# Ramp and tail orders, three moved steps and an idle TensorE, in a fused attention and expert kernel

## The reference

```
x = x + tanh(g_xattn) * (cross_attention(layernorm(x), ctx) @ Wo + bo)     # 16 heads of 8, 120 keys
h = rms(layernorm(x)) ;  q, k = rms per head of h @ wq.T, h @ wk.T ; v = h @ wv.T
y = layernorm(x) + causal_attention(q, k, v) @ wo.T   (features 0..31 of the attention part are zero)
gates = the top 2 of 4 of softmax(rms(y) @ gate_w.T), made to sum to 1
x = x + tanh(g_ffn) * (y + sum over 4 experts of gate * expert(rms(y)))    (features 0..31 of the experts are zero)
```

## Time and profile before

| | us |
|---|---|
| median of three executions (lowest, highest) | 1125.39 (1122.77, 1125.41) |
| the profiled execution | 1120.12 |
| its span, first to last instruction | 1118.4 |
| TensorE (PE) busy | 1010.6, 90% |
| VectorE (DVE) busy | 806.0, 72% |
| ScalarE (ACT) busy | 734.0, 66% |
| GpSimd (POOL) busy | 334.9, 30% |
| steps -1, 0, 1 begin at | 0, 34.6, 67.6 |
| step 2 and the loop begin at | 103.3, 160.3 |
| one round of the loop | 64.1 |
| steps 15, 16, 17, 18 begin at | 931.8, 994.5, 1054.8, 1098.6 |

### The profile page before, as it was taken

How to read it: one execution, slowest core, us unless ns; L and a number is a source line. 1 busy time by engine, 2 the same in 40 slices (tenths; PEclk the granted TensorE clock), 3 DMA queues, 4 the chain that set the end, 5 groups by cost and what they waited for, 6 DMA issues and landing times.

```text
span 1118.4 us, 25981 instructions
## 1 busy us (share of the span) xinstructions
PE 1010.6 (90%) x8578; PEld 622.6 (56%) x8578; DVE 806.0 (72%) x2170; ACT 734.0 (66%) x1331; POOL 334.9 (30%) x458
## 2 busy tenths in 40 slices
PE   3657799999999999999999999999999999998897
PEld 1334456656565655656565565655565565555454
DVE  7457777777877777787778777787777778655423
ACT  3455667676776766677676667768676767765453
POOL 6422314051422414151331405142241415132120
PEclk9979899999999999999999999999999999999899
DMA  6426533454433334454333344443333444403100
GB/s 193 111 48 185 142 94 71 117 126 123 126 104 98 101 85 111 123 126 123 100 102 87 87 122 126 123 121 102 97 92 89 125 123 112 118 9 93 33 10 10
DMA packets 77156, 114.26 MB, mean 102 GB/s; under 512 B 7616, under 2 KB 40000, under 8 KB 76992
## 3 DMA queue, kind: packets, MB, share of 16 engines
q1 hardware_dynamic: 76752, 111.54, 38.2%
q10 hardware_dynamic: 368, 2.24, 0.6%
HBM read 58.97 MB, written 53.74 MB: 101 GB/s over the span
## 4 chain that ended last, share of the span: by engine, by line
PE 56%; DVE 23%; ACT 10%; issue 8%; DMA 2%; POOL 0%; DVEq 0%; SPq 0%; ACTq 0%; POOLq 0%
PE ps_pv L1161 9%; PE ps_w L1187 7%; PE ps_s2a L1140 6%; PE ps_s2a L1198 5%; PE ps_s2b L1140 4%; PE ps_s2b L1205 4%; ACT probs L787 4%; DVE mpadB L915 4%; PE ps_t L1044 4%; DVE mpadA L915 3%; PE ps_w L1205 3%; PE ps_t L1174 2%; PE ps_w L1122 2%; PE ps_w L1118 2%; DVE ym L944 2%
## 5 line engine op out<-in xcount | busy, mean ns | idle before, releaser
L787 ACT ACTIVATE probs<-ps_s2a 120x512 f32<-120x512 f32 (+1 forms) x256 | 153.7, 600 | 92.3 <-PE ps_s2a L1140 86.8
L915 DVE TENSOR_REDUCE mpadB<-ps_w 128x4 f32<-128x512 f32 x256 | 158.6, 682 | 29.0 <-PE ps_w L1122 29.0
L915 DVE TENSOR_REDUCE mpadA<-ps_w 128x4 f32<-128x480 f32 x252 | 147.8, 649 | 36.7 <-PE ps_w L1122 36.6
L787 ACT ACTIVATE probs<-ps_s2b 120x512 f32<-120x512 f32 (+1 forms) x256 | 154.0, 602 | 0.0
L678 POOL TENSOR_SCALAR_AFFINE_SELECT probs<-probs 128x1024 f32<-128x1024 f32 x128 | 139.8, 1092 | 0.1
L1187 PE MATMUL ps_w<-W,hid 128*128 128x96 f32 x1024 | 130.0, 281 | 4.4 <-DVE split_k L821 1.1
L1187 PEld LDWEIGHTS ps_w<-W,hid 128*128 128x128 f32 x1024 | 122.2, 195 | 16.4 <-issue 13.5
L649 POOL TENSOR_TENSOR rB<-vrB,neg_half 128x4 f32<-128x4 f32 x16 | 16.1, 1007 | 374.1 <-DVE veB L814 374.1
L1140 PE MATMUL ps_s2a<-qdA,kstA 128*120 128x512 f32 x128 | 69.3, 541 | 14.9 <-issue 7.9
L944 DVE SCALAR_TENSOR_TENSOR ym<-ps_w,gates,ym 128x96 f32<-128x96 f32 x192 | 47.6, 310 | 43.6 <-PE ps_w L1187 43.5
L1198 PE MATMUL ps_s2a<-hid,W 128*128 128x512 f32 x160 | 78.4, 604 | 0.0
(11 more groups left out here) (202 smaller groups left out, 2086.4 us busy)
## 6 DMA issues: line engine op xcount, KB each, us to landing
scratch_Aq<-split_q SPq DMA_DIRECT2D x48, 256.0 KB, 2.4
qdA<-scratch_Aq SPq DMA_DIRECT2D x64, 192.0 KB
scratch_Bq<-split_q SPq DMA_DIRECT2D x48, 256.0 KB, 2.4
scratch_Bk<-split_k SPq DMA_DIRECT2D x48, 256.0 KB, 3.0
qdB<-scratch_Bq SPq DMA_DIRECT2D x64, 192.0 KB
kstB<-scratch_Bk SPq DMA_DIRECT2D x64, 192.0 KB
scratch_Ak<-split_k SPq DMA_DIRECT2D x48, 240.0 KB, 2.3
kstA<-scratch_Ak SPq DMA_DIRECT2D x64, 180.0 KB
```

Of the source, the lines that this page charges most:

```text
L787: nc.scalar.activation(probs[0:k, slot_of(part, *index), :], bank[0:k, :], ACT.Exp, scale=SCALE if part == "A" else 1.0).then_inc(done, 1)
L915: nc.vector.tensor_reduce(mneg[OP[part]][:, :, c, b], bank[:, 0:HT * k].rearrange("p (h k) -> p h k", h=HT), AX.X, ALU.max, negate=True).t ...
```

## The change

In the loop three works move. `base` becomes a work of A and goes from `first_experts` to the end of `self_attention`, so that it now runs for the group whose attention comes next in the same step; the load of x of the next group stands at the head of the step as before and waits for it. The context has a work of its own, `N ctx`, behind it. The 32-feature copy becomes `D keep`, behind gates 0 and one step earlier; it waits there for the store of the group before.

The stacks get another layout everywhere: load j fills every fourth partition, from j, and the row of maxima lies in partition 96 instead of 24.

The ramp and tail get new orders. In steps -1 and 0, x, context and base are done one group ahead. Step 0 transposes xn before the first exact product; step 1 starts with the exact products instead of hT. Step 15 has the last estimate of B and its mT sooner; step 16, formerly part of `SCHEDULE`, has a list of its own in which the four estimates of B stand among the experts' layers and the first expert layers of D come last; steps 17 and 18 are reordered and use other banks. Outside the loop VectorE makes the block-diagonal keys of B before the low part of the keys.

In step -1 alone TensorE multiplies the identity by itself into bank t, whose content nobody reads: 4 times behind each quad of estimates, 5 times ahead of mT and 12 times behind it.

The diff, cut to its core (old orders of steps 0, 1 and 17, and waits that follow from the orders, are left out):

```diff
-    return (one("N", "load", 0, None) + exact("D", 0, 0) + one("B", "hT") + down(1) + exact("D", 0, 2)
+    return (one("N", "load", 0, None) + one("N", "ctx", 0, None) + exact("D", 0, 0) + one("B", "hT") + down(1) + exact("D", 0, 2)
...
-            + values("D", 2) + one("D", "nT", 0, "t") + one("B", "root", 0, None))
+            + one("A", "base", 0, None) + values("D", 2) + one("D", "nT", 0, "t") + one("B", "root", 0, None))
...
-            + one("D", "gates", 0, None) + fill("D", "e1_w1", 1) + one("A", "oT", 1, "t") + fill("D", "e1_w2", 1)
+            + one("D", "gates", 0, None) + one("D", "keep", 0, None) + fill("D", "e1_w1", 1) + one("A", "oT", 1, "t") + fill("D", "e1_w2", 1)
...
-            + one("N", "base", 0, None) + fill("D", "e2_l1", 1) + fill("D", "e3_down", 0) + one("D", "gates", 1, None)
+            + fill("D", "e2_l1", 1) + fill("D", "e3_down", 0) + one("D", "gates", 1, None)
...
 def first_group():
-    return (one("N", "load", 0, None) + one("N", "stats", 0, None) + one("N", "norm", 0, None) + one("N", "base", 0, None)
+    return (one("N", "stats", 0, None) + one("N", "norm", 0, None) + one("A", "base", 0, None) + one("N", "load", 0, None)
             + one("N", "xT") + one("N", "q", 0, "f") + one("N", "k", 0, "f") + one("N", "v", 0, "pv")
-            + estimate("A", 0) + estimate("A", 1, "ffww") + estimate("A", 2, "wwff") + estimate("A", 3) + one("A", "mT"))
+            + estimate("A", 0) + estimate("A", 1, "ffww") + estimate("A", 2, "wwff") + estimate("A", 3) + one("A", "mT")
+            + one("N", "ctx", 0, None))
...
 def second_group():
+    return (one("N", "stats", 0, None) + one("N", "norm", 0, None) + one("N", "xT")
+            + exact("A", 0, 0) + exact("A", 0, 2) + one("N", "q") + exact("A", 1, 0) + one("N", "k") + exact("A", 1, 2)
+            + values("A", 0) + exact("A", 2, 0) + exact("A", 2, 2) + estimate("A", 0) + values("A", 1)
+            + exact("A", 3, 0) + one("A", "oT", 0, "t") + exact("A", 3, 2) + estimate("A", 1) + values("A", 2) + values("A", 3)
+            + one("A", "nT", 0, "t") + one("A", "oT", 1, "f") + one("A", "wo", 0, "t") + estimate("A", 2) + one("N", "v", 0, "f")
+            + one("A", "nT", 1, "t") + one("A", "wo", 1, "t") + one("A", "stats", 0, None)
+            + estimate("A", 3)[:2] + one("A", "norm", 0, None) + estimate("A", 3)[2:] + one("A", "mT")
+            + one("A", "base", 0, None) + one("N", "ctx", 0, None) + one("N", "load", 0, None))
...
 def third_group():
+    return (exact("A", 0, 0) + exact("A", 0, 2) + one("B", "hT") + exact("A", 1, 0) + exact("A", 1, 2)
+            + one("B", "qk", 0) + one("B", "qk", 1) + one("B", "qk", 2) + one("B", "qk", 3) + values("A", 0)
+            + exact("A", 2, 0) + one("B", "squares", 0, None) + exact("A", 2, 2) + values("A", 1) + one("B", "sums", 0, None)
+            + exact("A", 3, 0) + one("A", "oT", 0, "t") + exact("A", 3, 2) + one("B", "root", 0, None)
+            + values("A", 2) + one("B", "init", 0, None) + one("B", "copy", 0, None) + one("B", "scale", 0, None)
+            + values("A", 3) + one("A", "nT", 0, "t") + one("N", "stats", 0, None)
+            + one("B", "qT") + one("B", "kT") + one("A", "wo", 0, "t") + one("A", "oT", 1, "f") + one("B", "v", 0, "f")
+            + one("N", "norm", 0, None) + one("A", "nT", 1, "t")
+            + estimate("B", 0, "ffww") + one("A", "wo", 1, "t") + estimate("B", 1, "wwff") + one("N", "xT", 0, "pv")
+            + estimate("B", 2) + one("N", "q", 0, "t") + estimate("B", 3, "ffww") + one("A", "stats", 0, None)
+            + one("B", "mT") + one("A", "norm", 0, None) + one("N", "k", 0, "pv") + one("N", "v", 0, "t"))
...
+def last_queries():
+    order = of_parts("ABDM")
+    late = estimate("B", 3) + one("B", "mT") + one("A", "oT", 1, "t")
+    order = [use for use in order if use not in late]
+    at = order.index(("D", "fill", ("e1_w1", 1), "f"))
+    order = order[:at] + one("A", "oT", 1, "t") + estimate("B", 3) + order[at:]
+    at = order.index(("D", "fill", ("e2_l1", 1), "f"))
+    return order[:at] + one("B", "mT") + order[at:]
+def last_self_keys():
+    return (exact("D", 0, 0) + one("B", "hT") + down(1) + exact("D", 0, 2)
+            + one("B", "qk", 0) + one("B", "qk", 1) + one("B", "qk", 2) + one("B", "qk", 3)
+            + exact("D", 1, 0) + exact("D", 1, 2) + one("B", "squares", 0, None) + values("D", 0) + exact("D", 2, 0)
+            + one("B", "sums", 0, None) + exact("D", 2, 2) + one("B", "root", 0, None) + values("D", 1) + one("B", "scale", 0, None) + down(0)
+            + exact("D", 3, 0) + one("D", "oT", 0, "t") + exact("D", 3, 2) + one("B", "qT") + one("B", "kT")
+            + values("D", 2) + one("D", "nT", 0, "t")
+            + fill("M", "e2_l2", 0) + one("D", "wo", 0, "t") + estimate("B", 0) + fill("M", "e2_l2", 1)
+            + values("D", 3) + fill("M", "e3_up", 0) + one("D", "oT", 1, "t") + estimate("B", 1) + fill("M", "e3_up", 1)
+            + one("D", "nT", 1, "t") + fill("M", "e2_l3", 0) + one("D", "wo", 1, "t") + one("D", "out", 0, None) + estimate("B", 2)
+            + fill("M", "e2_l3", 1) + estimate("B", 3) + one("D", "squares", 0, None) + down(2)
+            + one("D", "norm", 0, None) + one("B", "init", 0, None) + one("B", "copy", 0, None) + one("B", "mT")
+            + down(3) + one("M", "store", 0, None) + one("D", "xfT") + one("B", "v") + one("D", "logits")
+            + fill("D", "e1_w1", 0, "w") + fill("D", "e1_w2", 0, "w") + one("D", "keep", 0, None)
+            + fill("D", "e1_w1", 1, "w") + fill("D", "e1_w2", 1, "w")
+            + fill("D", "e2_l1", 0) + fill("D", "e2_l1", 1) + fill("D", "e3_down", 0, "w")
+            + fill("D", "e0_up", 0, "w") + fill("D", "e0_up", 1, "w")
+            + one("D", "gates", 0, None) + one("D", "gates", 1, None) + one("D", "gates", 2, None) + one("D", "gates", 3, None))
...
 def last_self_values():
+            + exact("D", 2, 0) + exact("D", 2, 2) + values("D", 1)
+            + exact("D", 3, 0) + one("D", "oT", 0, "t") + exact("D", 3, 2) + fill("M", "e2_l2", 0, "w") + fill("M", "e2_l2", 1, "w")
+            + values("D", 2) + one("D", "nT", 0, "t") + fill("M", "e3_up", 0, "w") + one("D", "wo", 0, "t")
+            + values("D", 3) + fill("M", "e2_l3", 0) + one("D", "oT", 1, "t") + fill("M", "e2_l3", 1)
+            + one("D", "nT", 1, "t") + fill("M", "e3_up", 1, "w") + one("D", "wo", 1, "t")
+            + one("D", "out", 0, None) + one("D", "squares", 0, None) + down(2) + one("D", "norm", 0, None)
+            + down(3) + one("M", "store", 0, None) + one("D", "xfT") + one("D", "logits")
+            + fill("D", "e1_w1", 0, "w") + fill("D", "e1_w2", 0, "w") + one("D", "gates", 0, None) + one("D", "keep", 0, None)
+            + fill("D", "e1_w1", 1) + fill("D", "e1_w2", 1) + fill("D", "e2_l1", 0, "w") + fill("D", "e2_l1", 1, "w")
+            + one("D", "gates", 1, None) + fill("D", "e3_down", 0, "w") + one("D", "gates", 2, None)
+            + fill("D", "e0_up", 0, "w") + fill("D", "e0_up", 1, "w") + one("D", "gates", 3, None))
...
 def last_experts():
+    return (fill("M", "down", 1, "t") + fill("M", "e2_l2", 0) + fill("M", "e2_l2", 1) + down(0) + fill("M", "e2_l3", 0) + fill("M", "e2_l3", 1)
+            + fill("M", "e3_up", 0, "w") + fill("M", "e3_up", 1, "w") + down(2) + down(3) + one("M", "store", 0, None))
...
-AHEAD = {"s1": (-1, 0), "mT": (-1, 0)}
-RAMP = [(-1, "N", first_group()), (0, "NA", second_group()), (1, "NAB", third_group()), (2, "NABD", of_parts("NABD"))]
+AHEAD = {("A", "s1"): (-1, 0), ("A", "mT"): (-1, 0), ("N", "load"): (-1, 0), ("N", "ctx"): (-1, 0), ("A", "base"): (-1, 0)}
+RAMP = [(-1, "N", first_group()), (0, "NA", second_group()), (1, "NAB", third_group()), (2, "NABD", fourth_group())]
 LOOP = (3, NG - 1)
-TAIL = [(NG - 1, "ABDM", of_parts("ABDM")), (NG, "BDM", of_parts("BDM")), (NG + 1, "DM", last_self_values()), (NG + 2, "M", last_experts())]
+TAIL = [(NG - 1, "ABDM", last_queries()), (NG, "BDM", last_self_keys()), (NG + 1, "DM", last_self_values()), (NG + 2, "M", last_experts())]
...
-        M_ROW = HD * SPLIT
+        M_ROW = HD * SPLIT * HT
...
-                        at = slice(32 * j, 32 * j + rows)
+                        at = slice(j, M_ROW, HT)
...
+                        sp.wait_ge(xn_ready, g)
+                        sp.wait_ge(x1_base, g)
+                        load_x(g)
+                    elif (part, work) == ("N", "ctx"):
+                        if st.parts in ("N", "NA"):
+                            for b, v in st.drains([("N", "k", 0), ("N", "v", 0)]):
                                 sp.wait_ge(drained[b], v)
-                        sp.dma_start(ctT[:], ctxT[:, bass.ds(g * CT, CT)]).then_inc(ctx_loaded, 16)
+                        elif st.parts != PARTS:
+
+                            for b, v in st.settled("w", "t", "pv"):
+                                sp.wait_ge(drained[b], v)
+                        sp.wait_ge(kd_ready["A"], g)
+                        load_ctx(g)
...
+            load_x(0)
```

(33 more changed lines are left out.)

59 lines of the change are left out of this document (14 added, 45 removed).

## The result

The changed kernel takes 1097.89 us (median of four executions, 1097.87 to 1100.51) against 1125.29 us (1122.77 to 1125.41); the ratio is 0.9768, with a 95% interval of 0.9748 to 0.9787. The profiled execution is 1097.87 us with a span of 1096.1, 22.3 less than that of before; it is against that one that the steps are compared. The time of the kernel before moves from set to set: in the three sets of runs behind the experiments its medians are 1122.7, 1121.9 and 1121.4. In what follows a "start" is that of a step's first exact (or, at the end, expert) product.

A forecast was written before the change was run, and what follows sets the result against it. TensorE was taken as the bound, busy for 1010.6 of 1118.4 us, with waits to remove. Loop -14.5, step 2's end -1.5, ramp -3 and tail -14 sum to -33: 1125.4 to 1092 us in the median, range 1080 to 1110.

The forecast's parts named there:

- The loop (16.0 with the end of step 2): Loop rounds: 1.21 us a round saved, times 12, -14.5 (bounds 0 and -15.5); step 2's end adds -1.5.
- the 1.5 of step 2's end: End of step 2: same collision as in a round, 0.9, plus 0.6 for low clock; -1.5 (bounds 0 and -3).
- The ramp (-3): Steps before the loop: step 2 starts at 100.3 instead of 103.32, -3 (bounds 0 and -7).
- I find its end only 1.3 us earlier than before, and the last estimates 2.5 earlier: Step 1, exact products first: the chain from hT to scale ends 1.3 us earlier, the last estimates come 2.5 earlier.
- The tail (-14): Steps 15 to 18: new orders remove waits and a slow stretch; sum -14.3, taken as -14 (bounds -6 and -20).
- Step 16: Tail: estimates between fills and D's first experts last remove waits and slow clock; -11.0, less 1.3 for ScalarE's switches, -9.7.
- Step 15: Tail: mTB comes sooner, removing one of the two waits on qdB; -1.6.
- Step 17: Tail: gains 2, as exact pairs and fills no longer wait for each other's banks.
- Step 18: End of the tail: gains 1 of the 3.9 us that its 19.8 have without TensorE.
- The identity products, the layout and keep (0): Identity products in ramp: 0 (bounds 0, +1); stack layout: no loop gain; keep: 0 (bounds 0 and 1 us a round).
- the new orders outside the loop give nothing: Rival: ramp and tail chains stay as long and waits reappear under other names; 1109 us, chance 0.08.

The follow-up runs named there:

- e2: Kernel before the change, with base in the loop replaced by GpSimd writes of constants and a one-column product: 1114.58 us against 1122.68.
- e1: Changed kernel with only step 1 in its old order: 1093.45 us.
- e8: e1's kernel with 73 more identity products in TensorE's waits in steps 0, 1, 2 and 17: 1087.42 us.
- e11: Changed kernel, step 1 in its new order, with e8's added identity products in steps 0, 2 and 17 only: 1094.49 us.
- e9: Changed kernel with steps 15 to 18 in the orders and banks of before: 1107.12 us.
- e3: Changed kernel with only step 17 in its old order and banks, keep behind gates 0: 1098.43 us.
- e4: Changed kernel without its 33 identity products: 1099.36 us.
- e5: Changed kernel with the stacks laid out as before: 1099.23 us.

## Why the prediction was right, and where it was not

*The loop (16.0 with the end of step 2): right.* It measured 16.8. L1010 and L1013 fell to 0.17, base and L899 did not meet, the load of x was in time, and e2 shows why L1010 was slow: GpSimd's reading beside a VectorE instruction with two SBUF inputs. It is worth 0.47 us a round there, of the 1.33 that the change gives (64.10 to 62.77). The rest goes with hb and L1013, as the trace after has neither beside a GpSimd instruction; no run moved base alone. One slip: the 1.5 of step 2's end lie behind the loop's first exact pair, so they belong into the loop's length and not ahead of its start. The first round, in which they lie, takes 64.0 after and took 66.2 before, so they were 2.1.

*The ramp (-3): wrong, +3.7.* At the start of step 2, for which the -3 was said, the change was 2.1 us behind, and step 2 added 1.6. Up to step 1 the steps held: maxima of step 0 at 45.4 (44.5 forecast), step 1 at 64.8 (63.4). The step that failed is "I find its end only 1.3 us earlier than before, and the last estimates 2.5 earlier". The chain of B ended later, not earlier: its last maximum at 101.74 against 99.66 before. I had moved the chain back by the exact products and not asked what ScalarE and VectorE do ahead of it in the new list: the root stands behind the last exponentials, and the norm of N and nT stand ahead of the first estimate. e1 shows it: with the old order the maxima start 6.3 us earlier, and the median is 4.4 lower. The other part is the clock, which I had taken as a gain or nothing: with the old order it is 0.65 in the second half of step 1 where before had 1.00, and e8, with it kept up, has that step 4.4 us shorter. How the loss divides between order and clock stays open, as the two move together (e11). In step 2 the table load at its start (1.28) and the clock (0.92 against 0.94) are what the traces show; no run takes them apart.

*The tail (-14): too large, -9.2.* Step 16 was right (-10.1 for -9.7), and e9 shows its waits and its clock as the cause. Step 15 gave 0.7 for 1.6: its wait on qdB is gone, but a wait of 1.4 on hid is new, and its old order takes 0.4 less (e9). Step 17 was the miss, +1.7 for -2: its order gains nothing (e3), the wait on xf went from 1.2 to 2.1 us, and behind it TensorE runs six microseconds at 0.50. Step 18 gave 0.1 for 1. All three were taken from waits and idle time without a chain that says what would end them.

*The identity products, the layout and keep (0): right,* each for the reason given: VectorE's maxima bound step -1 (e4), the factor on GpSimd hid the loads (e5). Keep was not tested by itself; no loss shows where it now stands. Step 0 began at 34.45; the forecast had the root right and put the first product 0.4 too early.

*The sum.* -33 against -22.3 between the profiles, of which the ramp is 6.7, the tail 4.8 and the loop -0.8. Between the medians it is 27.4. The other 5.1 us are in no step: before's one profiled execution was that much faster than its median, and its later medians (1121.4 to 1122.7) lie between. So part of how near 1092 came to 1097.89 is luck with that median, and the range of 1080 to 1110 was wide enough for a ramp with the wrong sign and a tail that gave a third less. The rival "the new orders outside the loop give nothing" was half true, of the ramp.

## What to carry to other kernels

Before a chain is moved back in a hand-written order, list for every engine what now stands ahead of it, not only for the engine that was to be fed. A wait of TensorE costs more than its length where the clock falls behind it: look at the granted clock of the stretch after the wait, and put idle products there rather than where another engine sets the pace. When two engines meet at a fixed place in each round, the instruction that suffers may be tiny and the price is that of what is queued behind it.

## What was not expected of the hardware

- The same code gets a different granted clock from run to run. e3, e5 and e9 have the ramp of the changed kernel but for the edit, and their loops start at 166.0, 165.4 and 166.0 us, not at 164.0; in e3 step 2 has a clock of 0.88, after 0.92. By the Trainium skill (TensorE: Matmul & The Clock Gate, "What's actually happening") the throttled state is the default and activity releases it; e4 and e8 agree, with 0.58 against 1.00 and 0.75 against 0.95.
- Plain writes by GpSimd leave a tiny scalar_tensor_tensor at 0.17 us and stretch a tensor_scalar group from 1.12 to 1.76 (e2).
- e4's rounds are 62.91 us and the changed kernel's 62.77, with the same loop body. That stays open.
